# Batches 1 to 7 of a mixed attention and expert kernel: one hardware loop on every engine, against a written-out sequence with constant waits

## The reference, cut to what matters

```
x = x + gate(project(attention(rotate(conv_qk(ln(x))), conv_v(ln(x)))))
t = tokens(x)
t = t + mixture_of_8_experts_top_2(ln(t))
```

## Time and profile before

| | us |
|---|---|
| median of 3 runs | 3048.92 (3046.03 to 3050.79) |
| the profiled execution | 3044.3 |
| its span, first to last instruction | 3042.6 |
| PE busy | 2841.2 (93%) |
| DVE busy | 2269.0 (75%) |
| ACT busy | 1469.0 (48%) |
| POOL busy | 1395.8 (46%) |

### The profile page before, as it was taken

The page is one execution under the profiler, slowest core; times in us unless marked ns, Lnnn a source line. Parts: engine busy times, 40 slices in busy tenths (PEclk is TensorE's granted clock), DMA queues, the critical chain, the costliest instruction groups (busy, mean ns, idle before and its releaser), DMA issues.

```text
span 3042.6 us, 54782 instructions
## 1 busy us (share of the span) xinstructions
PE 2841.2 (93%) x20238; PEld 2665.9 (88%) x20238; DVE 2269.0 (75%) x3470; ACT 1469.0 (48%) x1884; POOL 1395.8 (46%) x1056
## 2 busy tenths in 40 slices
PE   6999989998999899999999899989998999958996
PEld 5899889997999899988998899979997999847776
DVE  6677778777877787777877787778777887655663
ACT  2455435543555355534554355535553455435771
POOL 4244524543454434552464245443455246336883
PEclk9999999999999999999999999999999999969998
DMA  2555020102010210102010211020011111137665
GB/s 110 189 195 200 29 73 22 37 18 91 22 38 26 77 36 24 41 31 72 22 45 11 89 32 30 25 91 22 25 39 56 47 32 59 43 115 250 231 223 210
DMA packets 88838, 230.51 MB, mean 76 GB/s; under 512 B 17160, under 2 KB 17746, under 8 KB 88566
## 3 DMA queue, kind: packets, MB, share of 16 engines
q1 hardware_dynamic: 79478, 209.96, 20.5%
q0 software_dynamic: 9088, 16.94, 1.7%
HBM read 90.76 MB, written 96.89 MB: 62 GB/s over the span
## 4 chain that ended last, share of the span: by engine, by line
PE 73%; issue 7%; DVE 7%; POOL 4%; DMA 4%; ACT 3%; SPq 1%; DVEq 0%; POOLq 0%; ACTq 0%
PE PV L708 46%; PE ST L708 14%; PE MX L708 12%; DMA wt<-wall 2%; DVE rt L1417 1%; POOL acc L587 1%; DVE ul L1370 1%; ACT h L1100 1%; DMA qst<-stk 1%; DMA stk<-rt 1%; ACT xr L1100 1%; DVE mcol L1448 1%; POOL rt L580 1%; POOL E L595 1%; POOL E L593 1%
## 5 line engine op out<-in xcount | busy, mean ns | idle before, releaser
L587 POOL TENSOR_TENSOR acc<-acc,tmp 128x256 f32<-128x256 f32 x512 | 802.8, 1568 | 1282.6 <-DVE tmp L1463 1280.3
L708 PE MATMUL PV<-vh,El 128*128 128x258 f32 x4096 | 1189.7, 290 | 27.5 <-DVE vl L1443 22.1
L708 PE MATMUL PV<-vh,Eh 128*128 128x258 f32 x4096 | 1162.1, 284 | 0.0
L708 PE MATMUL PV<-vl,Eh 128*128 128x256 f32 x4096 | 1152.2, 281 | 0.0
L1100 ACT ACTIVATE Eh<-ST 128x1024 fp32r<-128x1024 f32 x512 | 526.2, 1028 | 765.1 <-PE ST L708 765.1
L1448 DVE TENSOR_REDUCE mcol<-MX 128x1 fp32r<-128x1024 f32 x512 | 625.8, 1222 | 313.4 <-PE MX L708 310.6
L708 PEld LDWEIGHTS PV<-vh,El 128*128 128x128 f32 x4096 | 777.6, 190 | 59.4 <-DVE vl L1443 20.5
L708 PEld LDWEIGHTS PV<-vl,Eh 128*128 128x128 f32 x4096 | 783.4, 191 | 25.5 <-issue 3.8
L708 PEld LDWEIGHTS PV<-vh,Eh 128*128 128x128 f32 x4096 | 777.4, 190 | 0.0
L1453 DVE TENSOR_TENSOR El<-E,Eh 128x1024 fp32r<-128x1024 f32 x512 | 635.2, 1241 | 0.0
L1100 ACT ACTIVATE E<-ST 128x1024 f32<-128x1024 f32 x512 | 522.2, 1020 | 0.0
(11 more groups left out here) (245 smaller groups left out, 3476.8 us busy)
## 6 DMA issues: line engine op xcount, KB each, us to landing
rows<-xr SPq DMA_DIRECT2D x68, 520.0 KB, 6.2
stk<-rt SPq DMA_DIRECT2D x64, 512.0 KB, 2.7
kst<-stk SPq DMA_DIRECT2D x192, 128.0 KB
qst<-stk SPq DMA_DIRECT2D x192, 128.0 KB
wt<-wall SPq DMA_DIRECT2D x39, 514.0 KB
wt<-wall SPq DMA_DIRECT2D x39, 512.5 KB
xrow<-rows SPq DMA_DIRECT2D x39, 260.0 KB
wall<-yrows SPq DMA_DIRECT2D x32, 256.0 KB, 4.6
```

What stands on the lines that cost most here:

```text
L587: nc.gpsimd.tensor_tensor(acc[:, ic, :], acc[:, ic, :], tmp[:, p, :], ALU.add).then_inc(s_acc, 1)
L708: return nc.tensor.matmul(o, w, m, start=start, stop=stop)
```

## The change

The five loops over batches 1 to 7 become Python loops, so that the seven batches stand one behind the other in each stream, and `b` is a number in all of them. Batch 0 is told apart by the new `first(b)`. The counts and the addresses of SP's transfers become constants. Batch 0 itself, its small `hp` loops included, and the expert stage are the same as before. The diff, with the parts that repeat left out:

```diff
+def first(b):
+
+    return isinstance(b, int) and b == 0
...
             def spilled(b, groups):
-                there = 16 * groups if isinstance(b, int) else sp.snap(b * 64 + 16 * groups)
+                there = b * 64 + 16 * groups
...
             def batch(b):
-                nxt = 1 if isinstance(b, int) else (b + 1) % B
-                ready = 1 if isinstance(b, int) else sp.snap(b + 1)
-                x_next = x_d[nxt, :, :] if isinstance(b, int) else x_d[sp.snap(nxt), :, :]
+                nxt = 1 if first(b) else (b + 1) % B
+                x_next = x_d[nxt, :, :]
...
-                if not isinstance(b, int):
-                    store_mid(b - 1, sp.snap(b * 2 - 1))
-                    wait(sp, s_mid, sp.snap(b * 32))
-                    wait(sp, s_rt, sp.snap(b + 0))
+                if not first(b):
+                    store_mid(b - 1, b * 2 - 1)
+                    wait(sp, s_mid, b * 32)
+                    wait(sp, s_rt, b + 0)
...
             batch(0)
-            with sp.Fori(1, B) as b:
+            for b in range(1, B):
                 batch(b)
...
             def batch(b):
-                prev = None if isinstance(b, int) else b - 1
+                prev = None if first(b) else b - 1
                 n = b * UNITS
...
             batch(0)
-            with pe.Fori(1, B) as b:
+            for b in range(1, B):
                 batch(b)
```

More of the change, by code:

```diff
@@ L451, in batch @@
                     stacks(b, h)
-                    if isinstance(b, int):
+                    if first(b):
                         for i in range((h - 1) * 10, min(h * 10, NROWS // FILL)):
                             fill(i)
-                wait(sp, s_xin, ready)
-                if not isinstance(b, int):
+                wait(sp, s_xin, b + 1)
+                if not first(b):
                     for i in range(2):
-                        wait(sp, s_sc[i], sp.snap(b * 16 * KC))
+                        wait(sp, s_sc[i], b * 16 * KC)
                 sp.dma_start(xt, x_next).then_inc(s_xt, 16)
             batch(0)
-            with sp.Fori(1, B) as b:
+            for b in range(1, B):
                 batch(b)
@@ L643, in _ @@
             batch(0)
-            with pool.Fori(1, B) as b:
+            for b in range(1, B):
                 batch(b)
@@ L1256, in _ @@
             batch(0)
-            with act.Fori(1, B) as b:
+            for b in range(1, B):
                 batch(b)
@@ L1692, in _ @@
             batch(0)
-            with dve.Fori(1, B) as b:
+            for b in range(1, B):
                 batch(b)
```

## The result

| | before | after |
|---|---|---|
| median of the runs on one chip, us | 3048.92 (3045.1 to 3050.79, 5 runs) | 3013.9 (3012.84 to 3020.63, 5 runs) |
| ratio | | 0.9893 [0.9879, 0.9907] |
| the profiled execution, us | 3044.3 | 3013.71 |
| its span, us | 3042.6 | 3012.0 |

The change is faster by 1.1%. The ratio is worked out from the single runs; the two medians differ by 35.0 us, and their quotient is 0.9885. The profiled executions differ by 30.6 us, near the forecast sum of 28.6, but not all of it lies where the forecast put it.

The account below looks back on a forecast made before the run. PE's stream was taken to bound the kernel, with 73% of the span. Jumps 15.0, PE's register additions 11.8 and additions in batch starts 1.8 us sum to 28.6 us, from median 3048.92 to 3020 us; range 3011 to 3033.

Parts of the forecast that it names:

- the split into two gains: Batches 1 to 7: removed loop jumps give 15.0 us, and register additions gone from PE's waits give 11.8 us.
- The jumps back: Batch ends: six taken loop jumps on five engines go, 2.5 us each, 15.0 us (12.9 to 17.3).
- I take 2.5 us, which is nearest to DVE's row: Start of a batch: cost of one jump, chosen between 2.88 us (first scores) and 2.15 us (second unit).
- The low end of the sum: Start of a batch: one jump costs 2.15 us, read at the second unit; 12.9 us for the jumps.
- DVE is the engine that counts: Start of a batch: DVE's 2.54 us idle delays the rotation feeding first scores; PE's own 1.81 us is partly covered.
- ACT, SP and POOL at nothing: Start of a batch: these engines wait for DVE's rotation anyway, so their jumps cost nothing.
- The register additions on PE: Units of batches 1 to 7: constant waits save 0.055 us a unit, more with layer norm; 11.8 us (9.5 to 13.4).
- The register additions in the starts: From rotation to first scores: about eight uncovered additions of 32 ns, seven starts, 1.8 us (0 to 4.2).
- Late code: Rival: PE's longer written-out code arrives late, 3.67 us a stop, two per batch; +23 us, 3072 us, chance 0.05.

Follow-up runs that it names:

- the kernel with registers kept: The kernel before with batches 1 to 7 written out, batch number still in a register on PE, DVE, ACT and POOL, SP constants: 3026.3 us, ratio 0.995.

## Why the prediction was right, and where it was off

The time was right (3013.9 in a range of 3011 to 3033, 3020 forecast), and so was the split into two gains; that the total came so near is in part luck, as the sum at the end of this part shows. Step by step:

*The jumps back*, forecast 15.0 us (12.9 to 17.3): **mis-sized**, 12.4 us measured, just under the low end, and 12.3 to 12.7 in the three other kernels that take them away or hide them. The step that failed is "I take 2.5 us, which is nearest to DVE's row". The first scores do come 2.7 us earlier, but at the second unit 2.1 us are left, and that is what a batch keeps. The low end of the sum, 2.15 from the earlier trace rows, was the right reading, since it lies further down the chain. What gives back the 0.6 us in between is not shown.

*DVE is the engine that counts*, PE's own stop being covered: right, and the runs show it from both sides. With DVE alone written out the whole 12.7 us came; with PE alone the starts gained nothing. ACT, SP and POOL at nothing: right.

*The register additions on PE*, forecast 11.8 us (9.5 to 13.4): right. The stretch from max_row of the fourth unit to the last values matmul repeats closely from batch to batch. Its two ends in PE's timeline, in batch 3 before and after:

```profile
1092.34 0.33 PE L708 MATMUL MX<-negid,mcol 128*128 128x128 f32 x2
...
1334.23 0.28 PE L708 MATMUL PV<-vh,Eh 128*128 128x258 f32 x1
```

```profile
1088.46 0.33 PE L712 MATMUL MX<-negid,mcol 128*128 128x128 f32 x2
...
1328.56 0.28 PE L712 MATMUL PV<-vh,Eh 128*128 128x258 f32 x1
```

That is 241.89 and 240.10 us. Over batches 1 to 7 of all 14 profiles it is 241.85 to 241.99 us in the eight whose PE reads registers and 240.08 to 240.14 in the six whose PE has constants, whatever the other engines read: 1.8 us a batch, 12.6 for seven.

*The register additions in the starts*, forecast 1.8 us (0 to 4.2): within its bounds. SP's first operand transfer, kst, is issued 36.01 us behind `conv_q` in an undisturbed batch, 36.13 with registers: 0.12 us, 0.8 for seven, as much as four additions of 32 ns where I counted eight. In that stretch of batch 3 the kernel with registers kept runs 43 register instructions on the line of `wait`, of 32 to 64 ns, together some 1.6 us, and the changed kernel none; the rest of the 1.6 us cost nothing that shows.

*Late code*, the rival on the slower side, did not come as forecast: in the view of waits PE has no idle time with "issue" as its releaser from 100 us to the end of batch 7. But fetched code did cost something, by another way: as a transfer. SP's timeline in batch 2 and in batch 3, from the last spill to the operands:

```profile
715.64 0.36 SPq L419 DMA_DIRECT2D stk<-rt  x1
719.89 1.25 SPq L412 DMA_DIRECT2D kst<-stk  x3
...
1039.79 0.36 SPq L419 DMA_DIRECT2D stk<-rt  x1
1042.59 1.25 SPq L412 DMA_DIRECT2D kst<-stk  x3
```

4.25 us against 2.80. The view of DMA in these two stretches shows the spill's 512 KB landing after 4.2 and after 2.7 us; one piece of code lies in the first stretch, none in the second.

```profile
q8 instruction: 1, 0.02, 1.8%
...
stk<-rt SPq DMA_DIRECT2D x1, 512.0 KB, 4.2
...
stk<-rt SPq DMA_DIRECT2D x1, 512.0 KB, 2.7
```

Spread evenly, the spill would put 32 KB on each of 16 DMA engines; 16 KB more on one of them, if a piece lies on one, would be an estimated half of 2.7 us, 1.35. The first scores of batch 2 came 42.77 us behind the last values matmul, those of batch 3 41.16. Batch 4 shows a smaller case: kst is issued 36.57 us behind `conv_q` in place of 36.01, in batch 2 37.44. Both fell on the same batches when the changed kernel was run again. With batch 0's small loops written out the pieces lie elsewhere, and the delay moved with them: in both such kernels kst is issued at 36.0 to 36.1 us in batches 2 and 4, but at 36.96 and 37.11 in batch 7, where a piece now lies beside the last spill. So the place is set by the program. The size is not fixed: in the changed kernel with 165 extra waits batches 2 and 4 lost 2.05 and 2.07 us. In the changed kernel the two make 2.0 us together, which no step of mine had. In batches 1 to 7 q8 carried 129 packets with 2.11 MB, 16.4 KB each; the late operands of batches 2 and 4, 1.43 and 0.56 us, are the delays beside a packet that the rows show.

*TensorE's clock* is in no step of mine either. In the start of a batch TensorE's granted clock is 0.89 to 0.93 of full speed, and how much differs between batches of one kernel; over the rest of batches 1 and 2 of the changed kernel it is 1.00. The view by stretch shows the first 75 us of batches 2, 3 and 6 of the changed kernel (busy us of PE, PEld, DVE, ACT and POOL, then the granted clock, the DMA share and GB/s):

```profile
682.33:757.33 75.00, 63.53 (x375) 56.11 (x374) 53.16 (x83) 21.62 (x33) 26.49 (x19) 0.91 0.28 92
1006.46:1081.46 75.00, 65.10 (x392) 57.73 (x391) 55.07 (x88) 22.31 (x34) 27.22 (x20) 0.93 0.28 92
1973.93:2048.93 75.00, 66.99 (x386) 59.48 (x385) 54.32 (x88) 22.10 (x34) 26.82 (x20) 0.89 0.28 92
```

It is 0.93 in batches 1, 3, 5 and 7, and in all seven of the kernel with registers kept; in batch 4 it is 0.91 as in batch 2. Batches 3, 5 and 7 take 322.1 to 322.2 us, where the kernel with registers kept takes 324.2 on the mean; batch 1 takes 322.5, batch 2 324.1, batch 4 323.2 and batch 6 322.8. Batch 6 has no late operands and is still 0.6 us longer, at the lower clock. How the loss of batches 2 and 4 splits between operands and clock is not shown.

The sum for batches 1 to 7 is 12.4 + 12.6 + 0.8 = 25.8 us, measured 22.8; the 3.0 us between them were lost ahead of the fourth unit, 2.0 of it seen as late operands. The forecast for this stage was 5.8 us too high: 2.6 in the jumps, 1.0 in the additions of the starts and these 3.0, less 0.8 that the additions of the units gave beyond their term. That the total still came to 30.6 is due to the expert stage, 9.5 us in the first pair of profiles and 5.6 in the second, on which the prediction had nothing. This made up for the 5.8, and that is luck.

## What to carry to other kernels

Where a hardware loop's body is long, look at the idle time behind its branch on every engine, and price the one whose first instruction of the next pass starts the longest chain; a hint on the loop took as much away here, 12.5 us, with one instruction more in each body. A wait on a register value costs a little each time it stands at the head of the bounding engine's line, 0.05 us here, and that adds up over units. Measure a gain at the latest point of the stage where it still shows, not at the first, and over a stretch that repeats from batch to batch.

## What the runs showed that was not expected

- A jump back with the hint: PE's branch 1432 ns in place of 3669, DVE's idle time behind it 0.38 us in place of 2.54, at 40 ns for the hint instruction.
- Fetched code shares the way with data here: with a 16 KB piece beside it a 512 KB spill landed after 4.2 us in place of 2.7, and the delay moved to another batch when the code moved.
- The granted clock in the first 75 us of a batch went from 0.89 to 0.93 within one kernel, and batches of the same stream took 322.1 to 324.1 us.
- A later stage with the same code took another time, 393 to 396 us in most kernels with PE written out against 399 to 406 with PE's loop; the cause is open.
- DVE's branch has a record of 62 ns before, and yet DVE stood idle for 2.54 us behind it, while the record of PE's branch holds its 3669 ns. The idle time behind a branch has to be read beside its record.
